# One instruction order per engine for all four batches, taken from a plan with durations and due times; attention scores as pairs on the two row halves of the array

## Chip, core and metric

The kernel runs on one core of one Trainium2 chip. The metric is the device time in microseconds (us) of one execution. The engines are TensorE (PE), VectorE (DVE), ScalarE (ACT), GpSimd (POOL) and SyncE (SP), which issues every DMA.

## What is computed

A pre-norm transformer layer on x of shape (4, 1024, 128): four batches of 1024 tokens. Cut to what matters:

```python
# attention: 16 heads of 8 over sums of keys ("sets" of 4, 8, ..., 1024 tokens) plus the token's own tail
qkv = layernorm(x) @ W_attn.T
K = k_cum[r] - k_cum[l - 1]; V = v_cum[r] - v_cum[l - 1]        # 64 sets for each 128 tokens
att_logits = where(t >= r_idx, q . K * scale, -inf); att_tail = q . K_tail * scale
att = softmax(concat(att_logits, att_tail))
x = x + (att[:-1] @ V + att[-1] * V_tail) @ W_proj.T
# feed-forward: 32 experts of 64 hidden, 6 chosen in 4 of 8 groups, and 256 shared hidden
h = square(relu(xn @ up_w.T)) * combine[expert]
x = x + h @ down_w + square(relu(xn @ shared_up.T)) @ shared_down
```

## The kernel before

Tokens lie in two windows of 512 per batch (w = 0, 1), heads in four groups of four (g). For each window and group there are these steps, and the names are used below:

- **max unit**: PE multiplies the queries of one tile of 128 tokens with all set sums of a head into PSUM (line 871). One matmul covers the sets that every token may see (51 rows: six 8-row pieces of the bf16 split, 3 constant rows), a second one the last 64 sets, with 64 staircase rows more that mask what is ahead (115 rows). DVE reduces the row maxima (line 1088). After a group's last one, DVE merges them with the tail's logit (line 1102), POOL splits them in three bf16 parts (lines 574 to 577), PE turns them (line 880), DVE copies (line 1095), and a DMA puts them as three more rows into QA (line 533).
- **exp unit**: PE multiplies again with sets as output rows (line 912) into two PSUM banks, ACT takes the exponential of 1024 columns (line 729).
- **PV step**: PE multiplies with the values (line 929); four heads lie side by side, each in 32 columns of the array.
- **post chain**, once for each window: out of PV over the projection, second layernorm, logits (line 843) and expert choice to the combine weights (cT), a long row of small DVE operations (lines 1132 to 1202).
- **FFN unit**: a chunk of 128 hidden rows of the 18 (16 routed, 2 shared), for each window: up by three matmuls (line 972), the combine weights spread over 128 partitions by a further matmul (line 980), relu on ACT (line 757), relu times weight on DVE (line 1239), times relu again on POOL (line 656), down into one accumulating bank (line 991). 36 units per batch.
- **prep** of a batch: first layernorm, q, k, v (line 800), the sums over sets, splits into bf16 parts, which are stored to DRAM and loaded into QA and KA in 8-row pieces (lines 483 to 501).

What sets the order: `attention_order()` writes one list for one batch from a small model of durations, and each engine walks it. It holds all attention events of the batch and the post chain of window 0. After it, `ffn()` runs 36 slots in a fixed form; the post chain of window 1, the prep of the next batch and its first max groups are put into slots by tables (`POST_AT`, `PREP_AT`, `LEAD_AT`). Batches 0 to 2 are a hardware loop (`Fori`), batch 3 is written out. So attention and FFN of a batch follow each other: no FFN unit stands among attention units. All the single-bank steps (mT, oT, aT, proj, xT, logits, cT, yT) share one PSUM bank, `misc`.

SP issues DMAs in program order, as every engine does; a DMA waits behind what SP still waits for.

Of the kernel before, what the change touches and what calls it, by code (L numbers as in the profile page):

```python
# [18 lines left out]

# [27 lines left out]
ROW_PART = N_STAIR  # L47
ROW_CONST = ROW_PART + len(PART_PAIRS) * HS
# [6 lines left out]
MAX_UNITS = [[(3, 0, 2), (3, 2, 2), (2, 0, 2), (2, 2, 2), (1, 0, 4), (0, 0, 4)],  # L55
             [(i, h, 1) for i in (7, 6, 5, 4) for h in range(G)]]
# [10 lines left out]
NPT = 4  # L67


def numbering(units):  # L70
# [8 lines left out]
POST_STEPS = ["norm", "aT", "proj", "stats", "apply", "xT", "logits", "score", "pairs", "groups", "experts",  # L79
              "weights", "parts", "cT"]  # L80
UNITS = NW * NCH
LAG = 3
Y0_AT = NCH + LAG + 3
CHUNKS = [16, 17] + list(range(16))


POST_AT = {v: [step] for v, step in zip((0, 2, 3, 4, 5, 7, 8, 9, 10, 11, 12, 13, 14, 16), POST_STEPS)}


PREP_AT = {15: ["ln_stats"], 17: ["ln_apply0"], 18: ["ln_apply1"], 19: ["f0", "f1"], 20: ["f4", "f5"], 21: ["tails_k", "f2"],  # L90
           22: ["sums_k", "f3", "f6"], 23: ["ksplit", "f7"], 24: ["qsplit0", "tails_v"], 25: ["qsplit1"], 26: ["prod", "sums_v"],
           27: ["f11"], 29: ["f8", "f9", "f10"]}
PREP_ALL = [st for u in sorted(PREP_AT) for st in PREP_AT[u]]
FILL_ORDER = [st for st in PREP_ALL if st[0] == "f"]
FILLS = len(FILL_ORDER)
fill_no = {st: n for n, st in enumerate(FILL_ORDER)}

LEAD_GROUPS = 2
LEAD = []
for _g in range(LEAD_GROUPS):  # L100
    LEAD += [("max", 0, _g, n) for n in range(len(MAX_UNITS[0]))] + [("mfin", 0, _g, 0)]
    if _g == 1:
        LEAD.insert(len(LEAD) - 4, ("mT", 0, 0, 0))
LEAD_FROM = 30
LEAD_AT = {}
for _n, _ev in enumerate(LEAD):
    LEAD_AT.setdefault(LEAD_FROM + _n * 10 // len(LEAD), []).append(_ev)
FFN_SLOTS = max(UNITS + LAG, max(LEAD_AT) + 1)


POST_TIME = {"norm": (0, 3.4, 0.4), "aT": (0.9, 0.6, 0), "proj": (1.3, 0.8, 0.8), "stats": (0, 2.8, 1.6), "apply": (0, 1.1, 1.1),
             "xT": (0.9, 1.3, 0.7), "logits": (0.4, 0.3, 0), "score": (0, 1.2, 1.2), "pairs": (0, 1.3, 1.3),
             "groups": (0, 1.7, 1.7), "experts": (0, 1.7, 1.7), "weights": (0, 0.5, 0.5), "parts": (0, 2.5, 0), "cT": (0.3, 0.6, 0)}
MISC_STEPS = ("aT", "proj", "xT", "logits", "cT")
EAGER = 0.0
POST_GAP = 1.2


def attention_order():
# [1212 lines left out]
```

## Time and profile before

| | us |
|---|---|
| median of 3 runs (lowest, highest) | 1028.71 (1025.87, 1037.26) |
| the profiled execution, first to last instruction (span) | 1027.8 |
| PE busy | 864.9 (84%) |
| DVE busy | 518.4 (50%) |
| ACT busy | 317.2 (31%) |
| POOL busy | 278.3 (27%) |
| mean granted clock of TensorE, as a share of full speed | 0.815 |

The profile gives no time of its own for the profiled execution beside the span; the median of the unprofiled runs is 0.9 us above it. Busy time of PE is the union of its matmuls with modelled ends, so it shows where PE has work and not how fast it is: its clock stands beside it as a share of 2.4 GHz, and is at one of two levels (1.0 is 2.4 GHz, 0.50 is 1.2 GHz) at any moment. A line with "x4" merges four instructions; the number before the bracket of a wait is in microseconds.

### The profile page before, as it was taken

The page shows a single profiled execution, that of the slowest core. Times are in us where ns is not written, and L with a number is a line of the kernel's source. Part 1 is how long each engine was busy: PE and PEld are TensorE (multiplying, and loading weights), DVE is VectorE, ACT ScalarE, POOL GpSimd, SP SyncE. Part 2 cuts the span into 40 slices and gives each one's busy share as a digit, 9 for nine tenths or more (in the row PEclk, how much of TensorE's full clock was granted, in tenths as well). Part 3 has the DMA queues.
Part 4 walks back from the last instruction along what each step waited for, and adds up shares of the span by engine and source line. Part 5 has one row for each costly group of instructions (what it writes and reads, how often), then busy time and mean ns, then how long its engine had stood idle before and what let it go on. Part 6 is the DMA issues. An engine that isn't in the chain of part 4 may idle for free.

```text
span 1027.8 us, 13052 instructions
## 1 busy us (share of the span) xinstructions
PE 864.9 (84%) x3760; PEld 379.2 (37%) x3760; DVE 518.4 (50%) x1306; ACT 317.2 (31%) x435; POOL 278.3 (27%) x384
## 2 busy tenths in 40 slices
PE   3248999887778999987887899988786999997898
PEld 1223342243434333234443333324343433333444
DVE  2524575166824566327652455724772356552653
ACT  1202343532211233442421133353231123335232
POOL 1201010145522110114462111013445310111465
PEclk9655895799968778779987887778997768769999
DMA  9650000000251000000055000000005300000000
GB/s 188 158 61 7 2 1 1 1 22 0 54 77 33 2 1 2 1 21 1 1 82 67 13 2 1 2 1 21 0 31 70 49 12 2 1 1 1 1 1 20
DMA packets 29694, 26.05 MB, mean 25 GB/s; under 512 B 3164, under 2 KB 28828, under 8 KB 29500
## 3 DMA queue, kind: packets, MB, share of 16 engines
q1 hardware_dynamic: 29628, 25.21, 14.4%
q8 instruction: 36, 0.59, 0.3%
q14 instruction: 30, 0.25, 0.1%
HBM read 18.00 MB, written 6.82 MB: 24 GB/s over the span
## 4 chain that ended last, share of the span: by engine, by line
PE 54%; issue 16%; DVE 12%; DMA 9%; POOL 5%; SPq 2%; ACT 2%; DVEq 0%; POOLq 0%; ACTq 0%
PE mx L871 16%; PE om L929 13%; PE st L912 9%; DMA QA<-q_parts 6%; PE om L991 5%; PE st L972 3%; POOL PT L656 3%; DVE PT L1239 2%; PE om L938 2%; SPq L495 1%; PE om L843 1%; PE st L980 1%; DVE XN L1041 1%; PE mx L800 1%; ACT PT L729 1%
## 5 line engine op out<-in xcount | busy, mean ns | idle before, releaser
L1088 DVE TENSOR_REDUCE MXR<-mx 128x1 f32<-128x512 f32 (+6 forms) x352 | 202.0, 591 | 250.5 <-PE mx L871 247.2
L656 POOL TENSOR_TENSOR PT<-PT 128x512 f32<-128x512 f32 x144 | 183.3, 1279 | 296.4 <-DVE PT L1239 211.7
L871 PE MATMUL mx<-KA,QA 51*128 51x448 bf16 (+5 forms) x960 | 203.4, 266 | 50.6 <-DMA QA<-q_parts 43.8
L729 ACT ACTIVATE PT<-st 128x1024 f32<-128x1024 f32 x160 | 160.1, 1022 | 219.8 <-PE st L912 219.7
L871 PEld LDWEIGHTS mx<-KA,QA 51*128 51x128 bf16 (+1 forms) x960 | 92.8, 100 | 267.1 <-issue 200.6
L929 PE MATMUL om<-PT,VA 128*32 128x512 f32 (+1 forms) x768 | 166.4, 702 | 6.4 <-ACT PT L729 6.0
L991 PE MATMUL om<-PT,wdown 128*128 128x512 f32 x288 | 158.2, 633 | 1.3 <-POOL PT L656 1.3
L757 ACT ACTIVATE PT<-st 128x512 f32<-128x512 f32 x144 | 86.0, 597 | 222.9 <-PE st L972 220.1
L912 PE MATMUL st<-QA,KA 118*128 118x256 bf16 (+2 forms) x512 | 147.8, 361 | 4.9 <-ACT PT L729 3.0
L1239 DVE TENSOR_TENSOR PT<-PT,st 128x512 f32<-128x512 f32 x128 | 86.2, 683 | 64.6 <-ACT PT L757 54.0
L972 PE MATMUL st<-XH,WUH 128*128 128x512 f32 x144 | 102.6, 713 | 0.0
L980 PE MATMUL st<-CT,exp_sel 96*128 96x512 bf16 x128 | 52.8, 413 | 45.2 <-DVE PT L1239 45.2
L912 PEld LDWEIGHTS st<-QA,KA 54*128 54x128 bf16 (+1 forms) x512 | 47.0, 102 | 85.4 <-issue 49.5
L574 POOL TENSOR_TENSOR MS<-MALL,zeros 128x16 bf16<-128x16 f32 x32 | 7.3, 229 | 244.9 <-DVE MALL L1102 244.9
L991 PEld LDWEIGHTS om<-PT,wdown 128*128 128x128 f32 x288 | 58.4, 206 | 9.0 <-POOL PT L656 3.5
L972 PE MATMUL st<-XH,WUL 128*128 128x512 f32 x144 | 61.3, 426 | 0.0
L972 PE MATMUL st<-XL,WUH 128*128 128x512 f32 x144 | 60.9, 423 | 0.0
L735 ACT ACTIVATE OS<-om 128x512 f32<-128x512 f32 x32 | 19.1, 597 | 93.9 <-PE om L929 93.9
L1117 DVE COPY ATT<-om 128x144 f32<-128x144 f32 x32 | 9.8, 305 | 75.3 <-PE om L938 75.3
L980 PEld LDWEIGHTS st<-CT,exp_sel 96*128 96x128 bf16 x128 | 13.0, 101 | 89.1 <-DVE PT L1239 68.4
L972 PEld LDWEIGHTS st<-XL,WUH 128*128 128x128 f32 x144 | 29.9, 208 | 22.3 <-issue 22.0
L972 PEld LDWEIGHTS st<-XH,WUH 128*128 128x128 f32 x144 | 29.7, 207 | 22.4 <-issue 20.5
(134 smaller groups left out, 685.2 us busy)
## 6 DMA issues: line engine op xcount, KB each, us to landing
QA<-q_parts SPq DMA_DIRECT2D x48, 128.0 KB
q_parts<-Qparts SPq DMA_DIRECT2D x8, 384.0 KB, 11.2
KA<-k_parts SPq DMA_DIRECT2D x24, 128.0 KB
X<-in_x_dram SPq DMA_DIRECT2D x4, 512.0 KB, 3.9
QA<-in_q_stair_dram SPq DMA_DIRECT2D x1, 2048.0 KB, 23.1
out_dram<-Y SPq DMA_DIRECT2D x8, 256.0 KB, 3.0
k_parts<-Kparts SPq DMA_DIRECT2D x4, 384.0 KB, 2.5
PT<-in_up_dram SPq DMA_DIRECT2D x1, 1152.0 KB, 9.5
```

Of the source, the lines that this page charges most:

```text
L656: pool.tensor_tensor(H[:, u % 4, :], src[:, u % 4, :], R[:, u % 4, :], ALU.mult).then_inc(s_h, 1)
L729: act.activation(PT[:, k % NPT, h0:h0 + nh, 0:nt], src, ACT.Exp, scale=SCALE).then_inc(s_exped, 1)
L757: act.activation(R[:, u % 4, :], st[:, u % 2, :], ACT.Relu).then_inc(s_relu, 1)
L871: ins = pe.matmul(mx[:, u % 2, ns * k + s0:ns * k + s1], QA[r0:K_RAW, w, h, P * (i % WT):P * (i % WT) + P], KA[r0:K_RAW, h, s0:s1], start= ...
L912: ins = pe.matmul(st[:, 2 * (u % 2) + at // WIN, at % WIN:at % WIN + a1 - a0], KA[r0:K_SUB, h, P * c:P * c + P], QA[r0:K_SUB, w, h, a0 - W ...
L929: ins = pe.matmul(opsum[32 * h:32 * h + 32, t0 - WIN * w:t0 - WIN * w + nt], VA[:, c, G * g + h, :], PT[:, k % NPT, h, 0:nt], start=(c == ...
L938: ins = pe.transpose(misc[:, P * i:P * i + P], OS[:, P * i:P * i + P], ident[:, :])
L972: ins = pe.matmul(st[:, v % 2, :], wa[:, P * k:P * k + P], xa[:, WIN * w:WIN * w + WIN], start=(n == 0), stop=(n == 2))
L980: pe.matmul(st[:, 2 + routed % 2, :], exp_sel[:, k, :], CT[:, WIN * w:WIN * w + WIN], start=True, stop=True).then_inc(s_bc, 1)
L991: pe.matmul(opsum, wdown[:, CHUNKS[n], :], H[:, d % 4, :], start=(n == 0), stop=(n == NCH - 1)).then_inc(s_dn, 1)
L1088: dve.reduce_max(MXR[:, g, i, h0:h0 + nh], mx[:, u % 2, 0:ns * nh].rearrange("p (h s) -> p h s", s=ns), AX.X).then_inc(s_maxed, 1)
L1239: dve.tensor_tensor(V[:, u % 4, :], R[:, u % 4, :], st[:, 2 + routed % 2, :], ALU.mult).then_inc(s_vw, 1)
```

## The change

The whole program is written out from five lists, one for each engine, that `plan()` builds over all four batches. `work()` names every step with its engine, a duration, and what it stands behind. `plan()` picks, engine by engine, among the steps that could start within a tenth of a microsecond the one whose `due()` time is the earliest. PSUM banks are given out by the plan too: six banks as a ring (pairs for max, exp and prep; banks 4 and 5 singly for the small steps and for up), one bank for PV, one for down.

```diff
+STARTUP, PERIOD = 40.0, 105.0
+OFF = {"att0": 0.0, "att1": 55.0, "ffn0": 79.0, "ffn1": 192.0, "prep": -38.0, "post": -16.0, "max": -37.0}
+UNIT_T = 4.0
...
+    if kind in FFN:
+        w, n = divmod(name[2] if kind != "bc" else unit_of(name[2]), NCH)
+        return at + OFF[f"ffn{w}"] + n * UNIT_T - (2.0 if kind in ("dn", "had") else 0.0)
...
+            limit = max(min(x[0] for x in c), free[eng]) + AHEAD[eng]
+            pick = min((x for x in c if x[0] <= limit), key=lambda x: (x[1], x[0], str(x[2])))
```

Max units take heads in pairs. The even head's operands lie on partitions 0 to 63, the odd head's on 64 to 127, with the staircase as a small matmul of its own in front; each head of a pair has its own bank. Exp units are built in the same way.

```diff
-                for k in range(nh):
-                    h = G * g + h0 + k
...
-                    for r0, s0, s1 in ((ROW_PART, 0, ns - BLK), (0, ns - BLK, ns))[i == 0:]:
-                        ins = pe.matmul(mx[:, u % 2, ns * k + s0:ns * k + s1],
-                                        QA[r0:K_RAW, w, h, P * (i % WT):P * (i % WT) + P], KA[r0:K_RAW, h, s0:s1],
-                                        start=True, stop=True)
+                for k, (i, at, ns) in enumerate(parts):
+                    for q in range(nq):
+                        for e in range(2):
+                            r, h = HALF * e, 2 * g + q0 + q
+                            ins = pe.matmul(bank[:, e, at + ns * q:at + ns * q + ns],
+                                            QA[r:r + K_RAW, w, h, P * (i % WT):P * (i % WT) + P],
+                                            KA[r:r + K_RAW, b % 2, h, 0:ns], start=False,
+                                            stop=(k == len(parts) - 1 and q == nq - 1), skip_group_check=True)
```

The combine weights of a unit come by two DMAs from DRAM (64 partitions each, four buffers WB) in place of the matmul of line 980. ACT squares, DVE multiplies with the weights, POOL has no part in an FFN unit any more.

```diff
-                            pe.matmul(st[:, 2 + routed % 2, :], exp_sel[:, k, :], CT[:, WIN * w:WIN * w + WIN],
-                                      start=True, stop=True).then_inc(s_bc, 1)
...
+                for e in range(2):
+                    sp.dma_start(WB[HALF * e:HALF * e + HALF, n % NWB, :],
+                                 Cd[r // 16, 2 * (r % 16) + e].partition_broadcast(HALF)).then_inc(s_wb[n % NWB], 16)
...
+                    act.activation(rv, rv, ACT.Square).then_inc(s_sq, 1)
...
+                dve.tensor_tensor(H[:, m % NHB, :], RV[:, m % NRV, :], WB[:, r % NWB, :], ALU.mult).then_inc(s_had, 1)
```

Smaller parts: K, and Q of each window, are stored in DRAM in the order in which QA and KA are filled, so each piece is 8 rows of 8 KB, 12 pieces for each fill in place of 6; KA has two buffers; the 3 MB of staircase rows for QA and KA and the 384 KB of exp_sel are not loaded any more (QS and KS hold 48 KB for each half); x is loaded twice for each batch; POOL takes the sums of K in batches 1 to 3 and attn_out in both windows; the combine weights are no longer split in bf16 parts; q, k and v are filled and evacuated 1024 columns at a time.

The order on PE, in the attention of window 1. mx is the max unit's PSUM, st the exp unit's. Before:

```order
L871 MATMUL mx<-KA,QA 128x448
L871 MATMUL mx<-KA,QA 128x64
L912 MATMUL st<-QA,KA 128x256 x2
L858 REGISTER_ALU
L871 MATMUL mx<-KA,QA 128x448
L871 MATMUL mx<-KA,QA 128x64
L912 MATMUL st<-QA,KA 128x256 x2
L858 REGISTER_ALU
L871 MATMUL mx<-KA,QA 128x448
L871 MATMUL mx<-KA,QA 128x64
```

And now, at a like place in the middle of the program (L909 and L915 are a max unit, L932 and L937 an exp unit, L1009 up, L1021 down):

```order
L909 MATMUL ring<-KS,QS 128x64 x2
L915 MATMUL ring<-KA,QA 128x512 x2
L1009 MATMUL ring<-XH,WUH 128x512
L1009 MATMUL ring<-XL,WUH 128x512
L1009 MATMUL ring<-XH,WUL 128x512
L932 MATMUL ring<-QS,KS 128x256 x2
L937 MATMUL ring<-QA,KA 128x512 x2
L1009 MATMUL ring<-XH,WUH 128x512
L1009 MATMUL ring<-XL,WUH 128x512
L1009 MATMUL ring<-XH,WUL 128x512
```

Units of the FFN of an earlier half batch now stand between those of the attention. The end of PE's order is different: behind the last PV step of batch 3 stand 46 of the 144 up units, with their downs.

The order on SP. Before, inside the loop, from one batch's attention to the next batch's loads:

```order
L533 DMA QA<-MB 3x16x128
L477 ISA
L479 ISA
L479 DMA X<-in_x_dram 128x8x128
L482 REGISTER_ALU
L483 DMA k_parts<-Kparts 128x3x512
L486 REGISTER_ALU
L488 DMA q_parts<-Qparts 128x3x512
L498 ISA
L501 DMA KA<-k_parts 8x16x512 x6
L495 DMA QA<-q_parts 8x16x512 x6
```

And now, around the loads of batch 3 (WB<-combine are the weights of FFN units, two DMAs each):

```order
L617 DMA WB<-combine 64x512 x4
L606 DMA QA<-MB 3x8x128 x2
L573 DMA k_parts<-Kparts 8x16x512 x3
L648 DMA combine<-CT 32x512
L590 DMA q_parts<-Qparts 8x16x512 x3
L583 DMA KA<-k_parts 8x4096 x12
L600 DMA QA<-q_parts 8x4096 x12
L590 DMA q_parts<-Qparts 8x16x512 x3
L617 DMA WB<-combine 64x512 x6
```

The weights' DMAs stand among the maxima rows and the loads of the next batch: 64 of them for each batch, beside some 66 others.

## Rows read from the trace of the kernel before

**Rows 1.** The page: busy time of each engine, and granted clock in 40 slices.

```profile
PE 864.9 (84%) x3760; PEld 379.2 (37%) x3760; DVE 518.4 (50%) x1306; ACT 317.2 (31%) x435; POOL 278.3 (27%) x384
...
PEclk9655895799968778779987887778997768769999
```

**Rows 2.** Windows over one batch: stretch, its length, busy (instructions) of five engines, clock, DMA.

```profile
325.00:350.00 25.00, 22.59 (x117) 9.12 (x117) 12.67 (x27) 6.88 (x8) 3.67 (x13) 0.68 0.05 14
350.00:375.00 25.00, 25.00 (x141) 9.05 (x139) 15.30 (x32) 9.81 (x11) 2.07 (x5) 0.91 0.01 1
375.00:400.00 25.00, 24.66 (x112) 8.19 (x115) 13.50 (x37) 8.72 (x11) 2.97 (x6) 0.73 0.01 1
400.00:425.00 25.00, 25.00 (x102) 8.19 (x94) 15.58 (x60) 8.91 (x10) 3.03 (x9) 0.61 0.01 1
425.00:450.00 25.00, 21.21 (x113) 6.27 (x113) 2.95 (x8) 12.71 (x15) 1.93 (x5) 0.77 0.00 1
450.00:475.00 25.00, 21.82 (x93) 13.84 (x92) 14.59 (x32) 7.73 (x14) 11.61 (x10) 0.93 0.07 22
475.00:500.00 25.00, 16.79 (x57) 8.28 (x55) 20.01 (x76) 6.28 (x11) 12.19 (x10) 1.00 0.00 0
500.00:525.00 25.00, 19.96 (x66) 10.65 (x67) 19.70 (x34) 9.56 (x16) 11.89 (x11) 1.00 0.17 42
525.00:550.00 25.00, 16.98 (x57) 10.00 (x56) 4.62 (x7) 4.35 (x8) 10.70 (x16) 0.71 0.56 69
550.00:575.00 25.00, 23.80 (x95) 11.23 (x94) 11.62 (x22) 3.58 (x6) 8.79 (x12) 0.82 0.32 44
```

**Rows 3.** Waits: who waited for whom, total, times, longest.

```profile
DVE MXR L1088 <- PE mx L871: 247.2, 201, 25.2
...
ACT PT L729 <- PE st L912: 219.7, 111, 37.9
```

**Rows 4.** Timeline of attention at clock 1.00: start, us, engine, line.

```profile
357.79 1.24 PE L912 MATMUL st<-QA,KA 118*128 118x256 bf16 x6
...
358.96 0.79 PE L871 MATMUL mx<-KA,QA 51*128 51x320 bf16 x4
...
360.88 0.76 PE L871 MATMUL mx<-KA,QA 51*128 51x256 bf16 x4
...
361.58 1.05 PE L929 MATMUL om<-PT,VA 128*32 128x512 f32 x8
...
362.56 0.41 PE L871 MATMUL mx<-KA,QA 51*128 51x256 bf16 x2
```

**Rows 5.** Timeline of one FFN slot on PE at clock 1.00.

```profile
458.18 0.79 PE L972 MATMUL st<-XH,WUH 128*128 128x512 f32 x1
...
459.29 0.39 PE L980 MATMUL st<-CT,exp_sel 96*128 96x512 bf16 x1
...
459.51 1.02 PE L991 MATMUL om<-PT,wdown 128*128 128x512 f32 x2
...
459.97 0.80 PE L972 MATMUL st<-XH,WUH 128*128 128x512 f32 x1
```

**Rows 6.** Groups by form: busy us, mean ns, idle before.

```profile
L656 POOL TENSOR_TENSOR PT<-PT 128x512 f32<-128x512 f32 x144 | 183.3, 1279 | 296.4 <-DVE PT L1239 211.7 <-ACT PT L757 82.2 <-POOL TAIL L432 1.4
...
L1239 DVE TENSOR_TENSOR PT<-PT,st 128x512 f32<-128x512 f32 x128 | 86.2, 683 | 64.6 <-ACT PT L757 54.0 <-PE st L980 4.4 <-DVE cand L1182 1.4
L757 ACT ACTIVATE PT<-st 128x512 f32<-128x512 f32 x144 | 86.0, 597 | 222.9 <-PE st L972 220.1
```

**Rows 7.** DMA: the loads of QA in the chain that ended last.

```profile
528.18 21.05 DMA QA<-q_parts
```

**Rows 8.** Windows: the first 25 us, columns as in rows 2 (last: GB/s).

```profile
0.00:25.00 25.00, 8.27 (x17) 3.94 (x18) 6.33 (x28) 4.43 (x7) 4.42 (x13) 1.00 0.99 182
```

**Rows 9.** Tile QA: SP's issue of the maxima rows, ns min/median/max.

```profile
L533 SPq DMA_DIRECT2D QA<-MB x32: 698/707/927, 73.7 to 929.9; - x32
```

**Rows 10.** Timeline on PE alone, the first exp unit and what it waited for.

```profile
81.00 1.37 PE L912 MATMUL st<-QA,KA 118*128 118x256 bf16 x4 [1.91 <-DMA QA<-MB]
```

More of the change, by code:

```diff
@@ L77 @@
 pos_pv, PVN = numbering(PV_STEPS)
-POST_STEPS = ["norm", "aT", "proj", "stats", "apply", "xT", "logits", "score", "pairs", "groups", "experts",
-              "weights", "parts", "cT"]
+NPT, NRV, NHB, NWB = 3, 3, 4, 4
 UNITS = NW * NCH
-LAG = 3
-Y0_AT = NCH + LAG + 3
+ROUTED = NW * 16
 CHUNKS = [16, 17] + list(range(16))
[L87 to L92, printed above, removed]
@@ L108 @@
[L108 to L116, printed above, removed]
@@ new lines, in pv_step @@
+            def pv_step(b, w, g, k):
+                c, t0, nt, need = PV_STEPS[w][k]
+                m = (b * NW + w) * NG + g
+                if k == 0:
+                    if (w, g) == (0, 0):
+                        pe.wait_ge(s_evac, N("evac", b, "s"))
+                    if m:
+                        pe.wait_ge(s_oevac, m)
+                pe.wait_ge(s_expa, N("expa", b, w, g, need - 1))
+                for h in range(G):
+                    ins = pe.matmul(opsum[32 * h:32 * h + 32, t0 - WIN * w:t0 - WIN * w + nt],
+                                    VA[:, c, G * g + h, :], PT[:, pv_number(b, w, g, k) % NPT, h, 0:nt],
+                                    start=(c == 0), stop=(c == 2 * w + 1), skip_group_check=True)
+                ins.then_inc(s_pv, 1)
@@ new lines, in turn, with post @@
+            def turn(bank, of):
+                for i in range(WT):
+                    ins = pe.transpose(bank[:, P * i:P * i + P], of(i), ident[:, :])
+                return ins
+            def post(kind, b, w):
+                bank_free(kind, b, w)
+                bank = single(kind, b, w)
+                if kind == "aT":
+                    pe.wait_ge(s_ao, N("ao", b, w))
+                    turn(bank, lambda i: AO[:, WT * w + i, :]).then_inc(s_at, 1)
+                elif kind == "proj":
+                    if (b, w) == (0, 0):
+                        pe.wait_ge(s_w2, 16 * N_OTHER)
+                    pe.wait_ge(s_ate, N("aTe", b, w))
@@ L1301, in layout @@
     head_sel = np.repeat(np.eye(NH, dtype=np.float32), HS, 0)
-    exp_sel = np.zeros((3, NE, 16, P), np.float32)
-    for e in range(NE):
-        exp_sel[:, e, e // 2, 64 * (e % 2):64 * (e % 2) + 64] = 1.0
     return {
```

1681 lines of the change are left out of this document (832 added, 849 removed).

## The prediction

> **What bounds the kernel now.** I read the busy times first [rows 1]: PE is busy 84% of the span, the next engine, DVE, 50%. Then the waits [rows 3]: the two longest of DVE and ACT (247 and 220 us) are waits for PE. Then the windows over one batch [rows 2]: in 350 to 425 us, the attention, PE is idle 0.34 us of 75 and is the bound outright, but its clock stands at 0.91, 0.73 and 0.61. In 475 to 525, the FFN, the clock is 1.00 and PE is idle 13.25 us of 50, while DVE is busy 39.7. At 525 to 550 the core waits for the next batch's loads: DMA share 0.56, one piece of 21.05 us in the chain [rows 7]. So a batch of 250 us has PE work all the way, at half clock for a large part of the attention, and idle time in the FFN and at the batch's border.
>
> What PE would need at full clock: busy time times clock over the ten windows of rows 2 is 15.4 + 22.8 + 18.0 + 15.3 + 16.3 + 20.3 + 16.8 + 20.0 + 12.1 + 19.5 = 176 us for each batch.
>
> **What the change does to PE's work.** All per batch, at full clock.
>
> - Max units. Before, 240 matmuls. At clock 1.00 four of them, each with its weight load, take 361.58 - 360.88 = 0.70 us [rows 4], so 0.175 each: 42 us. The order now has 224 (96 staircase, 128 main), as 112 pairs on the two row halves. If the halves of a pair run side by side, a pair costs what one matmul did: 112 x 0.175 = 19.6. If not, 39. No row shows row halves. The nearest shows column strips: eight PV matmuls, four strips each, take 362.56 - 361.58 = 0.98 us [rows 4], 0.49 for four of 256 columns, where one f32 down of 512 columns takes 1.02 with its end [rows 5]: four strips cost what one matmul would. I take 19.6: saves 22.4.
> - Exp units. Before, 128 matmuls: 96 of 256 columns at (358.96 - 357.79) / 6 = 0.195 [rows 4], 32 of 512 at 0.22 (the 512-column bf16 matmul of line 980, 459.29 to 459.51 [rows 5]): 25.8 us. Now 144 in 72 pairs, 32 of 256 columns and 40 of 512: 15.0 side by side, 30 if not. I take 15.0: saves 10.8.
> - The spreading matmul: 32 x 0.22 = 7.0 us gone.
> - Changes of tile shape. The order has 418 changes between full array, row halves and column strips over the run, where before it was about 232 (only PV is in strips). Two max matmuls right behind the strips are followed by the next strips 0.35 us after their start, 2 x 0.175: I see no gap. Price between 0 and 0.06 us each (the 0.98 for eight strips leaves no more): 0 to 3 us a batch. I take 3.
>
> 176 - 22.4 - 10.8 - 7.0 + 3 = 139 us, say 140. Up and down stay as they are: a slot is 459.97 - 458.18 = 1.79 us [rows 5] with the spreading matmul's 0.22 in it, so a unit now costs PE 1.57 us.
>
> The Trainium skill bears on both of the first two lines. "TensorEngine Tiling (Array Packing)", section Tiling Modes, says that different tiles can load weights and multiply in parallel, and that a change of mode drains the array. By the first the pairs run side by side, as I assume from the strips. By the second each change would show the end of the matmul ahead: a matmul of 0.39 us is followed 0.22 after its start when nothing changes [rows 5], so a drain is worth at most 0.17 us, and 186 more changes would cost 32 us for the run rather than the 12 I count, 20 more in the sum. The strips in rows 4 show no such gap.
>
> **Other engines.** ACT gets 144 squares at the 597 ns of its relu [rows 6]: 317 + 86 = 403 us. POOL loses the 183 us of line 656 [rows 6] and keeps 95 and what it takes over from DVE. DVE keeps the product with the weights at 683 ns [rows 6], reduces the same columns, and hands K's sums and attn_out to POOL, which I count at nothing: at most 518. All are under PE's 560. SP issues about 130 DMAs a batch instead of 31, at up to 0.71 us [rows 9]: 92 us a batch, well under a batch's 150 to 160, but in order; a maxima row can stand behind a weights DMA that still waits for its buffer. The weights move 256 KB a unit. At the 182 GB/s of the start [rows 8] that is 1.4 us a unit and lies beside PE's 1.57 and the attention in between.
>
> **The clock.** Attention alone has a mean of 0.75 in 350 to 425, FFN 1.00 [rows 2]. Both at PE full of work, so it is not idling that lowers it there: it is what kind of matmul runs. It falls where 51- and 54-row matmuls follow each other for a while. Now FFN units stand in between, and pairs fill both halves. If attention's 54 us of the 140 (19.6, 15.0, and 19.6 for PV, 40 times 256 columns of four strips at 0.49) kept 0.75 and the rest 1.00, the mean would be 140 / (54 / 0.75 + 86) = 0.89. With the better filling I take 0.92. Bounds: 1.00, and 0.815, today's mean.
>
> **The sum.**
>
> 1. To the first exp unit: 81.0 us now [rows 10]. The 3.4 MB of staircase rows and exp_sel that are dropped are 19 us at 182 GB/s [rows 8]; the 21 us loads of QA [rows 7] go from 1 KB to 8 KB rows, some of which helps here too. I take 58.
> 2. PE work behind that: 4 x 140, less the 15 done by then, 545 us at full clock, 592 at 0.92.
> 3. PE idle in the mixed part: 0.34 of 75 us in attention, 13.25 of 50 in FFN [rows 2]. A mixed order should lie between 0.5% and 26%. Since there are always two kinds of work to choose from but the order is fixed beforehand, I take 10% of the time: 66 us. The border wait of a batch is covered by FFN units of the batch before, which have nothing to do with the loads.
> 4. The end: 46 up units stand behind the last PV step, 72 us of dense PE work that is inside 2, and covers the last post chain. Pipeline start and the last transpose, add and store: 9 us.
>
> 58 + 592 + 66 + 9 = 725 us of span, and with the 0.9 us between span and median 726.
>
> **The rivals.**
>
> *The clock stays.* The mean is 0.815 as now: 545 / 0.815 = 669, and 58 + 669 + 66 + 9 = 802. For it: more changes of shape and short waits on every engine. Against: 1.00 throughout 475 to 525 although PE was idle 26% there. The Trainium skill ("TensorE: Matmul & The Clock Gate", HAM oscillation) ties the low clock to idle gaps; by it alone the attention in 350 to 425 should have been fast, and rows 2 show it was not.
>
> *The halves don't run side by side.* Max and exp then cost 39 + 30 instead of 34.6: 34 us a batch more, 138 in all, 150 at 0.92, so 875.
>
> *The queues hold each other up.* The order is right for the durations in the plan alone. Where a DMA or a chain on DVE is late, the engine waits although other work is ready. If the whole mixed part has the FFN's idle share of 26% instead of 10%, 592 / 0.74 - 592 = 208 in place of 66: 867. If half of that, 796. I give this case 800.
>
> *The weights' DMAs set the pace: slower than before.* QA's six pieces of 128 KB take 21.05 us [rows 7], 3.5 each; a unit needs two such, 7.0 us, with four buffers of prefetch that hide latency but not rate. 128 units: 898 us behind the first combine weights, which come half a batch after the first exp unit, 58 + 77 = 135, and 10 for the end: 1043. It decides from about 7 us a unit on. Against: those pieces went to 8 partitions in 1 KB rows, the weights go to 64 in 2 KB rows, and the start moves 182 GB/s [rows 8], among it the same kind of spreading of staircase rows.
>
> *It doesn't do what it says.* Units of a half batch are to be spread behind its routing. The order shows that they are, in the middle, but 46 remain for the end. As PE has work all along this costs nothing, if PE is the bound: no rival of its own.
>
> **Chances.** My sum 0.62, the clock stays 0.13, queues 0.14, halves 0.07, the weights' DMAs 0.04. The predicted time is that of the first, 726 us. With clock 1.00 and 5% idle it would be 58 + 545 + 29 + 9 = 641; both at their best is unlikely, so I begin at 665. Upward the range takes in the clock's case and the queues', and part of the way to the halves': 850. A measurement tells about 1% from no change. Faster by over 1%: 0.95, within 1%: 0.01, slower by over 1%: 0.04.
>
> **What would show it.** Right: first exp unit near 58 us; mean clock over 0.9, with short stretches at half clock; a pair of 512-column score matmuls starting every 0.2 to 0.25 us; PE busy 88 to 92% between 60 us and the end; an FFN unit of 1.57 us in the last 72 us. Wrong: a clock of 0.5 over whole batches; the two halves of a pair starting 0.2 us apart; DVE's product waiting for DMA WB<-combine by the microsecond, many times; PE idle over a quarter behind releases by DVE; SP busy with issues without a pause.

## The result, and the profile after

The changed kernel takes 706.78 us (median of 4 runs, 698.44 to 712.56), the kernel before 1030.13 us beside it (4 runs, 1025.87 to 1037.26): a ratio of 0.687 with a 95% interval of 0.681 to 0.693. The forecast was 726 us. Medians are of all executions; without those that ran longer at a lower clock, the changed kernel's is 706.0 us and the largest difference this makes below is in the price of the pairs, 91 us in place of 101. The profiled execution has a span of 705.6 us and a mean granted clock of 0.923.

The page: busy times, and the clock in 40 slices of 17.6 us, which answer to [rows 1].

```profile
PE 578.2 (82%) x3632; PEld 278.1 (39%) x3632; DVE 443.3 (63%) x1079; ACT 385.6 (55%) x559; POOL 125.6 (18%) x275
...
PEclk9755799979999999889999999589999989999999
```

PE's share of the span is as before (82% and 84%). Its busy time fell by 287 us, through fewer and paired matmuls and a faster clock; idle time fell only from 163 to 127 us. Half-clock slices are left at the start (35 to 70 us) and around 450 us.

Windows in the middle of the run, and the mixed part as a whole; columns as in [rows 2].

```profile
300.00:350.00 50.00, 42.86 (x305) 18.06 (x304) 36.64 (x74) 26.57 (x40) 8.62 (x18) 0.93 0.31 70
350.00:400.00 50.00, 48.90 (x231) 25.91 (x229) 35.71 (x95) 31.30 (x53) 5.87 (x12) 1.00 0.35 98
400.00:450.00 50.00, 41.02 (x266) 18.68 (x264) 30.13 (x87) 33.02 (x44) 17.45 (x33) 0.93 0.33 77
...
68.04:696.60 628.56, 549.16 (x3466) 260.63 (x3467) 406.76 (x1001) 374.06 (x546) 109.01 (x237) 0.95 0.31 80
```

Attention and FFN now stand in the same windows. The last row is the prediction's middle part, from the first exp unit to 9 us before the end: PE is busy for 549.16 us and idle for 628.56 - 549.16 = 79.40, at a clock of 0.95.

Waits, which answer to [rows 3], with PE's longest and the one for the weights.

```profile
ACT PT L781 <- PE ring L937: 114.6, 58, 23.8
...
DVE MXR L1123 <- PE ring L915: 91.6, 41, 20.7
...
PE ring L909 <- issue: 30.2, 3, 13.9
...
DVE H L1222 <- DMA WB<-combine: 6.0, 3, 5.2
```

Waits for PE remain the long ones. DVE hardly waits for the weights' DMAs. The three waits of line 909 stand ahead of the first max unit of batches 1 to 3, as the timeline of PE shows:

```profile
155.84 0.29 PE L909 MATMUL ring<-KS,QS 64*128 64x128 bf16 x2 [11.23 <-issue]
...
289.22 0.29 PE L909 MATMUL ring<-KS,QS 64*128 64x128 bf16 x2 [5.04 <-issue]
...
458.30 0.29 PE L909 MATMUL ring<-KS,QS 64*128 64x128 bf16 x2 [13.94 <-issue]
```

The profile names no releaser here. The loads of K and Q of the next batch are what lands just before: ahead of these rows the chain that ended last has `137.21 7.84 DMA KA<-k_parts`, and loads of KA of 4.46 us at 280.87 and of 8.89 us at 438.77, and SP issues the Q loads from 146.48 to 150.47 us.

Timeline of PE at clock 1.00, for [rows 4, 5]: one pair of 512-column score matmuls with its staircase pair, and a slot of the FFN near the end.

```profile
303.90 0.28 PE L932 MATMUL ring<-QS,KS 64*128 64x256 bf16 x2
304.02 0.38 PE L937 MATMUL ring<-QA,KA 54*128 54x512 bf16 x2
...
688.40 0.79 PE L1009 MATMUL ring<-XH,WUH 128*128 128x512 f32 x1
689.03 0.39 PE L1009 MATMUL ring<-XL,WUH 128*128 128x512 f32 x1
689.27 0.40 PE L1009 MATMUL ring<-XH,WUL 128*128 128x512 f32 x1
689.50 1.02 PE L1021 MATMUL sums_ps<-H,wdown 128*128 128x512 f32 x2
689.96 0.79 PE L1009 MATMUL ring<-XH,WUH 128*128 128x512 f32 x1
```

Two 512-column matmuls together last 0.38 us, as one did before (0.39 for line 980 in rows 5). The FFN unit takes 689.96 - 688.40 = 1.56 us.

One thing more can be read from the starts on PE: what a change of tile shape costs, from full tiles (more than 64 rows) to row halves or to column strips and back. The same up matmul at clock 1.00, first with a row-half matmul behind it, then with a full one:

```profile
351.90 0.40 PE L1009 MATMUL ring<-XH,WUL 128*128 128x512 f32 x1
352.23 0.20 PE L909 MATMUL ring<-KS,QS 64*128 64x64 bf16 x2
...
353.12 0.40 PE L1009 MATMUL ring<-XH,WUL 128*128 128x512 f32 x1
353.35 1.02 PE L1021 MATMUL sums_ps<-H,wdown 128*128 128x512 f32 x2
```

The next matmul starts after 0.33 us in place of 0.23, so this change costs 0.10. The other frequent kinds of change, in both directions, cost 0.08 to 0.10 in this trace and in that of the kernel before.

Groups by line, for [rows 6]: busy us, mean ns, idle before.

```profile
L953 PE MATMUL sums_ps<-PT,VA 128*32 128x512 f32 (+1 forms) x768 | 94.0, 569 | 10.7 <-ACT PT L781 10.4
L1222 DVE TENSOR_TENSOR H<-RV,WB 128x512 f32<-128x512 f32 x128 | 88.9, 701 | 76.5 <-ACT RV L792 68.1
...
L792 ACT ACTIVATE RV<-RV 128x512 f32<-128x512 f32 x128 | 79.7, 629 | 2.6
```

The PV matmuls (line 953, the kernel before's line 929) are as many as before, 768, of the same size, and kept PE busy for 166.4 us then and 94.0 now: what eight strips in 0.98 us [rows 4] make for 768 of them at clock 1.00. These matmuls no longer run at half clock for much of the time.

### The profile page after: what moved, and what is told of

Read it like the earlier page. It is cut to its first block, busy times and chain, and to the rows that moved or that the text cites. A ratio compares the mean times of both kernels' runs of the same rounds, so it can differ in the third digit from the quotient of the medians.

```text
span 705.6 us, 10787 instructions
## 1 busy us (share of the span) xinstructions
PE 578.2 (82%) x3632; PEld 278.1 (39%) x3632; DVE 443.3 (63%) x1079; ACT 385.6 (55%) x559; POOL 125.6 (18%) x275
## 4 chain that ended last, share of the span: by engine, by line
PE 55%; DVE 13%; DMA 9%; ACT 8%; issue 8%; SPq 5%; POOL 1%; DVEq 0%; ACTq 0%; POOLq 0%
PE sums_ps L1021 16%; PE ring L1009 12%; PE sums_ps L953 9%; ACT PT L781 4%; PE ring L960 4%; DVE MXR L1123 3%; PE ring L937 3%; DMA KA<-k_parts 3%; PE ring L915 2%; PE ring L875 2%; SPq L583 2%; DVE H L1222 2%; PE ring L988 2%; PE ring L932 2%; PE ring L909 2%
## 5 line engine op out<-in xcount | busy, mean ns | idle before, releaser
L1123 DVE TENSOR_REDUCE MXR<-ring 128x4 f32<-128x1024 f32 (+2 forms) x192 | 176.3, 950 | 93.3 <-PE ring L915 91.6
L781 ACT ACTIVATE PT<-ring 128x1024 f32<-128x1024 f32 x160 | 159.2, 1022 | 115.4 <-PE ring L937 114.6
L1021 PE MATMUL sums_ps<-H,wdown 128*128 128x512 f32 x288 | 153.0, 625 | 8.6 <-DVE H L1222 8.3
L1222 DVE TENSOR_TENSOR H<-RV,WB 128x512 f32<-128x512 f32 x128 | 88.9, 701 | 76.5 <-ACT RV L792 68.1
L839 ACT ACTIVATE RV<-ring 128x512 f32<-128x512 f32 x144 | 85.0, 595 | 69.5 <-PE ring L1009 69.1
L953 PE MATMUL sums_ps<-PT,VA 128*32 128x512 f32 (+1 forms) x768 | 94.0, 569 | 10.7 <-ACT PT L781 10.4
L1009 PE MATMUL ring<-XH,WUH 128*128 128x512 f32 x144 | 87.8, 610 | 1.5 <-ACT RV L839 0.9
L909 PE MATMUL ring<-KS,QS 64*128 64x64 bf16 (+1 forms) x384 | 39.6, 217 | 54.7 <-issue 30.2
L792 ACT ACTIVATE RV<-RV 128x512 f32<-128x512 f32 x128 | 79.7, 629 | 2.6
L1021 PEld LDWEIGHTS sums_ps<-H,wdown 128*128 128x128 f32 x288 | 48.3, 191 | 43.4 <-DVE H L1222 24.0
L915 PE MATMUL ring<-KA,QA 51*128 51x256 bf16 (+7 forms) x512 | 63.3, 311 | 0.0
L937 PE MATMUL ring<-QA,KA 54*128 54x512 bf16 (+1 forms) x384 | 61.8, 359 | 1.7 <-ACT PT L781 0.8
L909 PEld LDWEIGHTS ring<-KS,QS 64*128 64x128 bf16 x384 | 18.3, 98 | 112.3 <-issue 74.5
L1009 PE MATMUL ring<-XL,WUH 128*128 128x512 f32 x144 | 57.4, 399 | 0.0
L1009 PE MATMUL ring<-XH,WUL 128*128 128x512 f32 x144 | 57.2, 397 | 0.0
L1009 PEld LDWEIGHTS ring<-XH,WUH 128*128 128x128 f32 x144 | 27.4, 190 | 33.7 <-issue 26.3
L932 PE MATMUL ring<-QS,KS 64*128 64x256 bf16 (+1 forms) x192 | 31.8, 327 | 10.2 <-DMA QA<-MB 5.1
L1009 PEld LDWEIGHTS ring<-XL,WUH 128*128 128x128 f32 x144 | 27.6, 191 | 15.1 <-issue 14.2
L937 PEld LDWEIGHTS ring<-QA,KA 54*128 54x128 bf16 x384 | 19.0, 98 | 33.0 <-issue 14.0
```

Of the source, the lines that this page charges most:

```text
L781: act.activation(dst, src, ACT.Exp, scale=SCALE).then_inc(s_expa, 1)
L792: act.activation(rv, rv, ACT.Square).then_inc(s_sq, 1)
L839: act.activation(RV[:, m % NRV, :], single("up", b, *k), ACT.Relu).then_inc(s_relu, 1)
L909: pe.matmul(own, QS[r:r + HALF, P * (i % 2):P * (i % 2) + P], mask, start=(k == 0), stop=False, skip_group_check=True)
L915: ins = pe.matmul(bank[:, e, at + ns * q:at + ns * q + ns], QA[r:r + K_RAW, w, h, P * (i % WT):P * (i % WT) + P], KA[r:r + K_RAW, b % 2, h ...
L932: pe.matmul(bank[:, e, 0:2 * P * nq].rearrange("p (q t) -> p q t", q=nq), KS[r:r + HALF, :], mask, start=True, stop=False, skip_group_chec ...
```

## Experiments

Each was timed beside the kernel before on the same chip, whose median lay between 1026.6 and 1034.2 us. That alone is a scatter of 0.7%, so a difference of a few microseconds between two of the new kernels can't be told from none.

**Pairs from one row half (one_half).** In max_unit and exp_unit both heads of a pair take their operands from partitions 0 to 63, so the odd heads' scores are the even head's; that part of the computation is left out.

```diff
-                        r = HALF * e
+                        r = 0
...
-                            r, h = HALF * e, 2 * g + q0 + q
+                            r, h = 0, 2 * g + q0 + q
```

> Both heads of a pair are taken from the lower row half (the odd head's scores are computed from the even head's rows, so its results are left out); banks, loads, order and counts stay. Side by side (my sum): pairs save 34.6 us of PE work a batch at full clock, 138 in all, so without them the time goes from 707 to 820 to 850 us, and a pair of 512-column matmuls no longer starts together but about 0.25 us apart. Rival, that the row halves never ran side by side or that weight loads and issue set the pace anyway: 700 to 714 us.

Measured: 808.18 us (792.68 to 832.09), 101 us more than the changed kernel and 12 under the expected range. PE busy 714.9 us, mean clock 0.862. The timeline of PE has the same pair again, one matmul behind the other:

```profile
331.94 0.60 PE L937 MATMUL ring<-QA,KA 54*128 54x512 bf16 x2
```

0.60 in place of 0.38: the halves do run side by side in the changed kernel, and that is worth 90 to 100 us. A part of it is the clock, 0.923 to 0.862. An estimate of the parts, from busy time times mean clock: PE's work at full clock is 714.9 x 0.862 = 616 us for 578.2 x 0.923 = 534, so 82 more, or 96 us of busy time at 0.862; the remaining 41 of the 137 us more of busy time are the lower clock. The time rose by less than 137, since PE's idle time fell from 127 to 85 us.

**Attention and FFN one after the other (seq).** The same instructions; a batch's up units wait for its last PV step, the next batch's exp units for its last down, and the due times are set to suit.

```diff
-            put(("up", b, u), "pe", 0.69, ("xle", b, w), ("wlow", 0), used, unit("dn", m - NHB))
+            put(("up", b, u), "pe", 0.69, ("xle", b, w), ("wlow", 0), used, unit("dn", m - NHB),
+                ("pv", b, NW - 1, NG - 1, len(PV_STEPS[1]) - 1))
...
```

> The same instructions, in an order in which no FFN unit of a batch stands before its last PV step, and no exp unit of the next batch before its last down unit, as in the kernel before. If FFN units among the attention are what lifts the clock: in attention it falls back to about 0.75 to 0.85, the mean from 0.92 to 0.86 or so, and the time rises to 735 to 760 us. Rival, that pairs on both row halves keep the clock up by themselves: mean 0.91 or more, and the time within 2% of 707.

Measured: 714.85 us (709.79 to 722.58), ratio 0.695 (0.685 to 0.706). Mean clock 0.941 in the profiled execution, higher than with the mixed order. The rival holds. Mixing the FFN's units among the attention, the idea behind the single order, is worth 8 us here, which is no more than the scatter (the two ratios' intervals overlap), and it isn't what lifts the clock.

**Both at once (seq_half).**

> The changed kernel with two of its parts undone at once: FFN units of a batch only behind its last PV step and the next batch's exp units only behind its last down (as in the run seq, 715 us), and both heads of a pair from the same row half (as in one_half, 808 us; the odd heads' scores are those of the even head's rows, so that part of the computation is left out). Theory, that the two effects simply add: 715 + 808 - 707 = 816, between 805 and 830, clock 0.86 to 0.89. Rival, that they help each other (with attention at the long, low-clock matmuls again and nothing of the FFN beside it, the clock falls as in the kernel before, 0.75 over the attention): score work of 69 us a batch rather than 35, at 0.75: above 850 us, mean clock 0.83 or less. What is then left to the 1031 of the kernel before is due to the rest: the FFN unit's chain, the merged matmuls, the loads.

Measured: 814.09 us (812.92 to 831.73), clock 0.855, against a sum of 816. Within the scatter the two effects add; the rival, above 850 us, is out. 216 of the 323 us between the kernels are still gained without them.

**The square back on POOL (pool_square).** DVE multiplies relu with the weights, POOL multiplies by relu again, ACT squares only the shared units.

```diff
-                put(("had", b, u), "dve", 0.72, ("sq", b, u), (("bc", b, routed_of(u)), 2.2))
+                put(("mul", b, u), "dve", 0.72, ("relu", b, u), (("bc", b, routed_of(u)), 2.2), unit("dn", m - NHB))
+                put(("had", b, u), "pool", 1.3, ("mul", b, u))
...
```

> The FFN unit's chain as before: ACT relu, DVE product with the weights, POOL times relu again (1.28 us each in the kernel before) in place of ACT's square, 128 units; the plan knows the step with 1.3 us. ACT loses 128 x 0.63 = 81 us, POOL gains 164 us (126 to 290 of 707). Theory, that PE bounds the kernel and other work covers a longer chain: within 2%, 700 to 721 us. Rival, that in the FFN stretches the unit's chain is what ends the wait (before, PE was idle 26% there and POOL busy 42 to 49%): POOL at 1.28 us beside DVE is near PE's 1.57 us a unit and also holds up the prep's sums and the splits of maxima, so the time rises by 20 to 60 us, to 727 to 767, with PE waiting for H by tens of us.

Measured: 748.73 us (745.25 to 756.78), ratio 0.733 (0.722 to 0.744): 42 us more, in the rival's range. Waits of PE in this kernel:

```profile
PE sums_ps L1028 <- POOL H L738: 29.6, 33, 5.2
```

In the changed kernel the same wait was 8.3 us, for DVE. A chain of relu 0.6, product 0.7 or more and POOL 1.27 us doesn't hide behind PE, although POOL is busy only 39% of the time. So that POOL leaves the FFN unit carries up to 42 us of the gain. Not all of it is the longer chain. In the groups of DVE by line, the product has become slower with POOL at work beside it, 952 ns for 701, 32 us in all:

```profile
L1229 DVE TENSOR_TENSOR H<-RV,WB 128x512 f32<-128x512 f32 x128 | 120.9, 952 | 63.4 <-ACT RV L846 55.5 <-DMA WB<-combine 5.1 <-PE sums_ps L1028 0.7
```

952 is a mean; the median is still 693. The 49 products that had no TENSOR_TENSOR of POOL beside them took at most 694 ns, the other 79 a mean of 1115 and up to 1774, as the second of these two:

```profile
709.52 0.69 DVE L1229 TENSOR_TENSOR H<-RV,WB 128x512 f32<-128x512 f32 x1 [4.68 <-DMA WB<-combine]
710.30 1.26 POOL L738 TENSOR_TENSOR H<-H,RV 128x512 f32<-128x512 f32 x1 [9.29 <-DVE H L1229]
710.68 1.42 DVE L1229 TENSOR_TENSOR H<-RV,WB 128x512 f32<-128x512 f32 x1 [0.47 <-DMA WB<-combine]
```

In the kernel before, where the weights came from PSUM, the product took 683 ns and at most 690, with POOL at work beside 47 of them [rows 6]. So this run is not quite that kernel's chain.

**The Q loads' delay in the plan (border).** 12 us (window 0) and 8 us (window 1) in place of 1.8 between the last Q load and the max units; the kernel's instructions are the same, their order is not.

```diff
-                        (("qld", b, w, PIECES - 1), 1.8))
+                        (("qld", b, w, PIECES - 1), 8.0 if w else 12.0))
```

> In the plan's durations only: the loads of Q land 12 us (window 0) and 8 us (window 1) behind their issue for the max units, in place of 1.8. PE stood idle 11.2, 5.0 and 13.9 us in front of the first max unit of batches 1 to 3. If that is the fixed order putting max units before the loads have landed while FFN units are ready: those 30 us shrink to under 8 and the time falls to 676 to 688 us. Rival, that the wait only moves, since the attention behind it comes later and ends later: 698 to 712.

Measured: 710.12 us (706.0 to 723.5), ratio 0.691 (0.684 to 0.698). No gain, as the rival had it, although of the 30.2 us of border waits 6.6 are left: the same line's waits for DVE rose from 10.8 to 25.4 us. The next kernel has the same delay in its plan.

**More plan numbers (tuned).** The delay above, the split of the up weights (line 1231, 3.6 us on DVE ahead of K's split) moved behind the first batch's preparation, and other due times, with 100 us in place of 105 between batches.

```diff
-OFF = {"att0": 0.0, "att1": 55.0, "ffn0": 79.0, "ffn1": 192.0, "prep": -38.0, "post": -16.0, "max": -37.0}
+OFF = {"att0": 0.0, "att1": 55.0, "ffn0": 79.0, "ffn1": 182.0, "prep": -33.0, "post": -26.0, "max": -32.0}
...
-    put(("whigh", 0), "act", 2.6, (("xload", 0), 20.0))
+    put(("whigh", 0), "act", 2.6, (("xload", 0), 20.0), ("prod", 0))
```

> Numbers of the plan alone: the Q loads' delay as the trace shows it (12 us for window 0, 8 for window 1, in place of 1.8), the split of the up weights behind the first batch's product (it stood ahead of the first batch's K split on DVE, 3.6 us), and due times found for these durations (FFN of window 1 10 us earlier, prep 5 later, post chain 10 earlier, max 5 later, 100 us between batches). Theory, that the border waits (30 us of PE in front of the first max unit of batches 1 to 3) and the late start are time that the order can give back: 680 to 700 us. Rival, that a wait taken away in one place comes back in another, as in the run border (710): 700 to 715, with the first exp unit some 3 us earlier at most.

Measured: 705.24 us (702.18 to 707.16), ratio 0.693 (0.688 to 0.699). No gain; the rival holds here too. Waits of PE:

```profile
PE ring L909 <- DVE MXR L1123: 18.3, 24, 8.9
...
PE ring L909 <- DMA QA<-q_parts: 9.4, 2, 6.0
```

The border waits of 30.2 us are gone from the list, and the same line's waits for DVE rose from 10.8 to 18.3. PE is busy 587.6 of 700.2 us, so idle 112.6 in place of 127.4: the idle time is less, but PE's work took 9 us longer for the same matmuls at the same mean clock. At the start SP issues the first Q load at 38.06 (41.41 before) and the second at 48.45 (53.86), and the first exp unit comes at 69.78 us, 1.7 later than in the changed kernel. The chain that ended last shows what is there instead:

```profile
53.59 1.66 POOL rstd L696
55.28 1.11 DVE XP L1071 x4
56.39 2.99 DVE MXR L1123 x5
```

The next batch's layernorm stands on DVE ahead of the maxima of this one.

**More work on SP (more_dma, tiny_dma).** Each unit's weights are brought again in part, into a buffer that nobody reads; 192 columns in the first kernel, 8 in the second. Bringing all 512 again was meant first, but two buffers of that size don't fit in SBUF, so that kernel has no time.

```diff
+                for e in range(2):
+                    sp.dma_start(WB2[HALF * e:HALF * e + HALF, n % 2, :],
+                                 Cd[r // 16, 2 * (r % 16) + e, 0:192].partition_broadcast(HALF)).then_inc(s_wb2[n % 2], 16)
```

> Behind the two weights DMAs of each FFN unit two more that bring 192 of the 512 columns again into a buffer that nobody reads (each waits for its own buffer's last fill): SP issues 256 DMAs more, about 0.65 us each, 166 us more of issuing, and 37.5% more bytes for the weights. Theory, that the weights' DMAs and their issue lie beside PE's work with slack: at most 1%, 700 to 714 us. Rival, that SP's queue is close to full, so that maxima rows and loads stand behind weights: 727 us or more, with exp units waiting for DMA QA<-MB and DVE's product for DMA WB<-combine by tens of us more than now (6.0).

Measured: 746.00 us (742.46 to 751.32), 39 us more.

> more_dma (746 us) with 8 columns instead of 192 in each of its 256 extra DMAs: the same extra instructions on SP, at 1/24 of the bytes. Theory, that it is SP's issuing (256 times some 0.6 us, 150 us) and the place in its queue that costs the 39 us: again 738 to 752. Rival, that it is the transport (12.6 MB more): then 705 to 715. With the waits: in the first case DVE waits for DMA WB<-combine about 60 us again, in the second about 6.

Measured: 739.22 us (734.06 to 746.66), 32 us more. Its waits of DVE:

```profile
DVE H L1233 <- DMA WB<-combine: 67.7, 38, 4.7
```

6.0 us in the changed kernel. The extra instructions took a median of 596 ns of SP each, 152 us in all, and almost all of the loss comes with them; the bytes of the larger version add 7 us, which can't be told from none. So SP, whose queue I had as covered, has little slack. The timeline of SP near the end shows where: with FFN units back to back SP issues without a pause (line 619 the weights, 624 the extra ones).

```profile
662.77 1.23 SPq L619 DMA_DIRECT2D WB<-combine  x2
664.05 1.24 SPq L624 DMA_DIRECT2D WB<-combine  x2
665.33 1.23 SPq L619 DMA_DIRECT2D WB<-combine  x2
```

A unit's four DMAs take 665.33 - 662.77 = 2.56 us, more than PE's 1.57 for the unit; the two of the changed kernel take half of that, which is less than 1.57. Some 32 units at 1 us more would be the 32 us, and 46 stand behind the last PV step (an estimate).

**One DMA in place of two (one_dma).** To take issuing away: a unit's weights in one DMA of 128 partitions.

```diff
-                for e in range(2):
-                    sp.dma_start(WB[HALF * e:HALF * e + HALF, n % NWB, :],
-                                 Cd[r // 16, 2 * (r % 16) + e].partition_broadcast(HALF)).then_inc(s_wb[n % NWB], 16)
+                sp.dma_start(WB[:, n % NWB, :],
+                             Cd[r // 16, 2 * (r % 16):2 * (r % 16) + 2].unsqueeze(1)
+                             .to_broadcast([2, HALF, WIN])).then_inc(s_wb[n % NWB], 16)
```

> The combine weights of an FFN unit by one DMA to 128 partitions in place of two to 64; the same bytes, the same order on every engine, 128 issues less on SP (some 0.6 us each, 76 us). Theory, that SP's queue already costs something in the changed kernel (more_dma lost 39 us to 166 us of extra issuing, so the slack is thin): 690 to 702 us. Rival, that the changed kernel lies just inside the slack and only more issuing hurts: 704 to 709. Third, that one DMA of 256 KB takes longer to land than two of 128 KB side by side, and more than the saved issue: above 710.

Measured: 1000.95 us (992.33 to 1002.98), 294 us more: the third case, but by far more than anything expected here. Tile WB: SP's issue in ns (min/median/max). Window and timeline near the end: columns as in [rows 2], then start, us, engine.

```profile
L616 SPq DMA_DIRECT2D WB<-combine x128: 486/3950/6942, 149.0 to 972.5; - x128
```

```profile
950.00:975.00 25.00, 16.77 (x25) 7.52 (x25) 3.39 (x5) 5.54 (x10) 0.00 (x0) 0.50 0.13 51
```

```profile
955.03 0.69 DVE L1222 TENSOR_TENSOR H<-RV,WB 128x512 f32<-128x512 f32 x1 [4.42 <-DMA WB<-combine]
960.16 0.69 DVE L1222 TENSOR_TENSOR H<-RV,WB 128x512 f32<-128x512 f32 x1 [4.43 <-DMA WB<-combine]
```

Products start every 5.13 us, 256 KB each, 51 GB/s. A DMA share of 0.13 is what 2 of 16 engines would show. The weights' DMAs now set the pace, as in the prediction's rival on them: the first exp unit and half a batch at 135 us, 128 units of 5.13 us and 10 make 802. It became 1001: from 149.0 to 972.5 us the weights' DMAs are issued one every 6.5 us in the mean. One cause of the difference is seen, that SP is held back in its other instructions as well: two of the maxima rows' DMAs, 1.56 us of issue in the changed kernel, took this long in the attention (timeline of SP):

```profile
396.73 7.47 SPq L606 DMA_DIRECT2D QA<-MB  x2
```

Whether that is all of it was not tested. The same DMA with tuned's plan numbers gave 1000.84 us (993.57 to 1002.25), where this was expected:

> The numbers of tuned (705 us) with the single DMA of one_dma. In tuned DVE waited 20.5 us for WB (longest 14.4) and the border waits had become smaller. If SP's queue was what gave that back: 680 to 695, the best of all. If not: 700 to 706.

**One DMA, spread evenly (even_dma).** The hidden rows of a chunk are laid out as expert 0, 1, 0, 1, ..., in both weights, so the source's outermost count is 64.

```diff
-                             Cd[r // 16, 2 * (r % 16):2 * (r % 16) + 2].unsqueeze(1)
-                             .to_broadcast([2, HALF, WIN])).then_inc(s_wb[n % NWB], 16)
+                             Cd[r // 16, 2 * (r % 16):2 * (r % 16) + 2].unsqueeze(0)
+                             .to_broadcast([HALF, 2, WIN])).then_inc(s_wb[n % NWB], 16)
...
+    mix = lambda a: a.reshape(NE // 2, 2, 64, C).transpose(0, 2, 1, 3).reshape(NE * 64, C)
```

> One DMA for each unit's weights again, but the rows of its source run row by row over the 128 partitions (expert 0, 1, 0, 1, ...; the hidden rows of a chunk are laid out in that order in the up and down weights), so that its outermost count is 64 and not 2. In one_dma (1001 us) a unit's DMA took 5.13 us at 51 GB/s with a DMA share of 0.13, which is 2 of 16 engines. Theory, that the outermost count of the DMA (2) set how many engines carry it, and not that it was one DMA: it lands in about 3 us as before, SP's issue is under 0.9 us a unit in place of 1.19, and the time is 690 to 704 (SP's queue has 40 to 76 us less in it, and tiny_dma lost 32 us to 150 us more). Rival, that one DMA to 128 partitions is slow by itself: 950 us or more again. Third, that it is even but SP's saved issuing is worth nothing: 704 to 710.

Measured: 702.83 us (696.73 to 711.24, 6 runs), ratio 0.685 (0.678 to 0.691). Tile WB:

```profile
L616 SPq DMA_DIRECT2D WB<-combine x128: 512/514/615, 152.4 to 688.8; - x128
```

It lands in 3.3 us (median). 298 us lie between two kernels that differ in the order of two dimensions of one DMA and in the layout of the weights that goes with it. It was not that it was one DMA; the order of the dimensions, and with it the outermost count, was the cause. Against the changed kernel, though, 4 us less can't be told from nothing (0.678 to 0.691 and 0.681 to 0.693): SP issues 514 ns for a unit in place of two times 594, 86 us less, and gets nothing measurable for it; where units stand back to back, SP was already faster than PE. The last try had tuned's plan numbers with it:

> The numbers of tuned (705 us) with the single, evenly spread DMA of even_dma. If SP's queue gave back what tuned won elsewhere (DVE waited 20.5 us for WB there): 680 to 695. If not: 700 to 706.

Measured: 707.16 us (703.56 to 716.91), ratio 0.690 (0.686 to 0.695), above both expected ranges. No version beat the changed kernel by more than a measurement can tell.

## Why the prediction was right

By the terms of the sum, predicted and measured (the window from 68.04 to 696.60 above):

| | predicted | measured |
|---|---|---|
| to the first exp unit | 58 | 68.0 |
| PE work behind it, at its clock | 592 (545 / 0.92) | 549.2 (522 / 0.95) |
| PE idle in the mixed part | 66 | 79.4 |
| the end | 9 | 9.0 (the window was laid so) |
| span | 725 | 705.6 |

The result lies 19 us under the forecast because PE work was 43 us less, and start and idle 10 and 13 more. That it is so near is in part luck, since errors of 10 and 13 us stand against one of 43. The end was not measured apart: the last down matmul ends at 700.7, 4.9 us before the end, so some of its 9 us belongs to the two lines above it.

- **Pairs.** Right in the mechanism: a pair costs what one matmul did, 0.38 us. The price of undoing them was too high: I had 138 us at full clock for the run, and one_half has 82 by the estimate above (and 91 to 101 in time).
- **Changes of shape.** This term was wrong, in count and in price. I counted 232 before, as if only PV changed the shape, and 418 after, at 0.03 us. But the kernel before goes from a 51-row tile to a 115-row one and back in every max unit. Counted over all matmul records of the two traces there are 1275 changes before and 442 after, and a change costs 0.08 to 0.10 us at full clock. I read "no gap" from the four max matmuls of rows 4: together they have 2 x (256 + 64) = 640 columns, which at 512 in 0.23 us would take 0.29, and they take 0.70. The four changes in them are the other 0.41; my 0.175 for each held a change of shape. So the change removes some 830 of them, by estimate about 75 us of PE's work at full clock, where I had added 12. This was hidden in the price of the max matmuls: between their starts and the next matmul's, weighed with the clock, the trace has 54 us for the max units over the run, where my 19.6 a batch made 78. That covers the 23 us by which PE work at full clock (522) lies below my 545. The Trainium skill ("TensorEngine Tiling (Array Packing)", Tiling Modes) says that a change of mode drains the array; both traces agree, with the 0.10 us above. No run changed the number of changes alone.
- **The clock.** The mean over the whole run is 0.923 and I had taken 0.92, but for the work behind the first exp unit, where it is 0.95; the agreement over the run is luck, made by 0.70 in the first 68 us. A reason was wrong as well. I gave two, FFN units in between and fuller row halves. seq takes the first away and has 0.941; one_half takes the second away and has 0.862, and seq_half, without either, 0.855. So of the two it is the pairs. They are not all of it: seq_half is still above the 0.815 of before. Low clock also stands where PE idles: 0.52 in 150 to 160 us and 0.50 in 450 to 460, around two of the border waits. The rule of the Trainium skill that ties the low clock to idle gaps ("TensorE: Matmul & The Clock Gate", HAM oscillation) fits these, and doesn't fit rows 2, where PE had no gap at 0.61.
- **Idle.** 79.4 of 628.6 us is 12.6%, for 10% predicted (PE busy 87%, for 88 to 92%). The step "the border wait of a batch is covered by FFN units of the batch before" failed. The plan gives a load 1.8 us; the trace has 8 us for a Q load in the chain ahead of the first exp unit and 4.5 to 8.9 for K. In a fixed order PE then stands at line 909, 30.2 us in all. border and tuned correct that number; most of the wait goes, and the time does not.
- **Start.** 58 was taken, 68.0 measured. I credited longer rows with faster loads. The K loads start at 36.9 us, the first max unit at 52.5, and the maxima from there to 68.0 need DVE, which I had not put in the sum. PE's order also has max units of window 1 ahead of the first exp unit, and the first of them waited 2.47 us for its Q load. tuned had Q loaded 3 to 5 us earlier and its first exp unit no earlier, with DVE's maxima and the next batch's layernorm in the chain.
- **Other engines.** ACT 386 (403 forecast), POOL 126 (95 and what it takes over), DVE 443 (at most 518). "All are under PE's 560" was right as a bound, but not as a price: pool_square shows that 166 us more on POOL, at 39% busy, cost 42 us. The share said nothing of the unit's chain, nor of the slower product beside it.
- **The weights' DMAs.** The rival had the right mechanism and the wrong form. 64 partitions in each DMA land in 3.0 us (median); PE covers them. Written as one DMA with 2 as outermost count they do set the pace, at 5.13 us a unit where FFN units stand alone, and the 7 us that I gave as the limit was too high: at 5.13 the kernel is already only 2.5% below the kernel before. SP's time I had only by the batch, 92 of 150 us; what counts is the unit, 1.2 us of issue beside PE's 1.57.

Where the 323 us came from, as far as runs tell: pairs 91 to 101, the square from POOL to ACT up to 42, mixing FFN and attention 8 (within the scatter), start 13 (81.0 to 68.0, from the traces). The remaining 160 or so were not taken apart further. Each price was taken by undoing that part alone; only pairs and mixing were undone together. In the 160 are the spreading matmuls (28 at full clock by rows 5), the fewer changes of shape (about 75 at full clock, estimated above), and the clock of the attention beyond what one_half undoes; how they share it is open. The waits ahead of the max units are not among them: 50.6 us at line 871 before, 54.7 at line 909 after.

## What to carry to other kernels

Ask of a changed order what the same instructions cost in a plain order, before you credit the order: here filling both row halves, and with it the clock, was worth some 100 us, and mixing the work about 8, which can't be told from nothing. When you take a matmul's price from a trace, look at the shape of the one ahead of it: the price may be that of the change. A low share of busy time doesn't mean that a step on that engine is free: its place in a unit's chain and what runs beside it count. When you merge DMAs, look at the outermost count of both sides, and at the DMA share of a window where little but that transfer runs.

## What the runs showed of the hardware

- A DMA with 2 as its source's outermost count ran at a DMA share of 0.13, 51 GB/s and 5.13 us for 256 KB; the same bytes with 64 outermost landed in 3.3 us (median). SP is then held back too: its issue of such a DMA took 0.49 us at least and a median of 3.95 us over the run, for 0.51 with 64 outermost. The Trainium skill ("DMA: Bandwidth & Descriptors", Why a DMA increments its semaphore by 16 and not by 1) has the rule, that a DMA runs on the largest number of engines up to 16 that divides the outermost count of both sides. That agrees with 2 engines here. It also agrees with the loads of K and Q, 8 rows each: in 38 to 42 us, where the core moves little else, the share is about a half, 8 of 16.

```profile
38.00:42.00 4.00, 3.83 (x18) 3.87 (x19) 0.02 (x1) 0.23 (x1) 0.00 (x0) 0.50 0.52 165
```

  A layout that lets these loads run at a higher share would aim at the border waits and the start. It wasn't tried.
- Two 512-column matmuls with 54 rows each, on the two row halves, took 0.38 us together and 0.60 from one half. Filling both halves raised the mean clock from 0.862 to 0.923 in the mixed order and from 0.855 to 0.941 in the plain one.
- A change of tile shape on TensorE (over 64 rows, 64 rows or fewer, column strips) cost 0.08 to 0.10 us at clock 1.00 from start to start. The kernel before has 1275 of them, the changed one 442.
- A DVE product of 128x512 f32 with both operands in SBUF took a mean of 1115 ns with a TENSOR_TENSOR of POOL beside it and 690 in the same run without. With one operand in PSUM it was 683, at most 690, with POOL beside it or not. The Trainium skill ("SBUF — State Buffer", Who interferes with whom) says that a product of two SBUF tensors contends with GpSimd's reads for a shared port; these numbers agree.
- In one_dma the FFN ran at clock 0.50 with one unit every 5.13 us; in the changed kernel the same matmuls back to back, PE busy 39.39 of the 40 us from 600 to 640, have 1.00.
- 256 DMA instructions of 596 ns more on SP cost 32 us, 128 fewer of them gained nothing that can be told. With FFN units back to back a unit's DMAs took SP 2.56 us in the one case and 0.51 in the other, against 1.57 for the unit on PE.
